# Output projection of the shared stage: three single-pass float32r products of 12-bit halves in place of one float32 product

## The chip, the cores and the metric

One Trainium2 chip, one of its cores. The metric is device time of that core in microseconds (us), the median of the runs shown.

## The reference

One transformer block over x of 2 x 2048 rows and 512 columns (T = 4096 rows):

```python
x = x + attention(layernorm(x))      # 4 x 512 rows, 8 heads of 16, causal
x = x + moe(layernorm(x))            # 8 experts of width 352, top 2, and one shared expert
# the end of attention: out [T, 128] -> out @ OUT_w.T + OUT_b, OUT_w [512, 128]
# the shared expert: silu(xt @ sw1) * (xt @ sw3) @ sw2, and scores = sigmoid(xt @ gate_w.T)
```

In the kernel's reading the batch is 2 x 2048. The change touches `out @ OUT_w.T` and nothing else of the arithmetic.

## The kernel before, in words

Every engine has its own program, written out by hand; they meet in semaphores. Four stages follow each other.

**Projections**, 8 chunks of 512 rows. Per chunk n: VectorE works out the row moments (`moments`, L1143: four BATCH_NORM_STATS2, then a chain of 14 small instructions that wait for each other, the last writes `shift`, L1149). ScalarE normalises with them (`normalise`, L709, four instructions of L714, each reads `shift`). TensorE transposes the normalised rows (`transposes`, L861, 16 instructions of L871), ScalarE copies them out (L722), TensorE projects (`project`, L878). VectorE's order within chunk n is `values(n-1)`, `moments(n+1)`, `rests(n-1)`, `rotate(n)`, `third_parts(n-1)`. In chunk 0 TensorE also transposes OUT_w into bank 3 (L894), and ScalarE copies that bank to `out_wt` (L767), between the Gelu of chunk 0 (L764) and `normalise(1)`; `s_wte` counts that copy, and `transposes(1)` wait for it.

**Attention**, in an order that a planner writes out (`attention_plan`). At its end the plan holds the heads of the next stage: HT (transpose an attention tile of 128 rows, L996, and copy it to `attn_t`, L803), HF (the output product of that tile, L1000, and VectorE's `front`) and HX, for tiles 0 to 2.

**Shared stage**, 32 steps, one for each tile of 128 rows. In step n TensorE does, in this order: `front(n+2)` (the output product, L1025: stationary `attn_t`, moving `out_wt`, 512 columns, bank 7), `turn(n+3)` (transposes the next attention tile, L1017, bank 0), `at(n-1)` (three transposes of the gated rows, L1034), `up(n)` (16 instruction records of L1051, 360 and 352 columns), `down(n-1)` (6 records of L1062). ScalarE: `to_copy(n+3)` (L821, bank 0 to `attn_t`; its semaphore `s_toe` is what `front(n+3)` and the next `turn` wait for), `at_copy(n-1)` (L814), Silu (L836). VectorE: `front(n+2)` (L1217: adds the product to the row of x, L1221 and L1222, its moments and the normalised row `xg`, L1228, some 17 instructions in a chain), `gated(n)` (L1325), `turn(n+1)` (L1214, the transposed tile `xg_t` that `up(n+1)` reads), in some steps a part of the choice of experts (`choose`, L1396 to L1410, in steps 9 to 11, 17 to 19, 25, 26, 28, 30 and 31) or `slots` (L1423 on, in steps 12, 20, 27, 29, 31), then `y(n-1)` (L1340). SyncE issues the transfers in its own order: the attention tile of row n+4 (L481), the normalised row to HBM (L485), a part of an expert's weights (L582 to L588), the same row back in four quarters (L493, after the write has landed), the result row (L577), the row of x (L573).

`x1` is a ring of XR = 6 rows of x; SyncE loads rows 0 to 4 during attention and then row n + XR - 1 in step n, after `y(n-1)`.

**Routed experts**, 71 blocks in a loop, with TensorE busy nearly throughout.

What the change touches, as it stands before:

```python
nc.scalar.copy(out_wt[:, :], psum[:, 3, :]).then_inc(s_wte, 1)                       # L767
nc.scalar.copy(attn_t[:, k % 2, :], psum[:, 0, HP:]).then_inc(s_toe, 1)              # L821
nc.tensor.matmul(psum[:, 7, :], attn_t[:, k % 2, :], out_wt[:, :], start=True, stop=True).then_inc(s_op, 1)   # L1025
```

Of the kernel before, what the change touches and what calls it, by code (L numbers as in the profile page):

```python
# [7 lines left out]
B, S, D = 2, 2048, 512  # L8
# [3 lines left out]
E, H = 8, 352  # L12
TOP_K, ROUTED_SCALE = 2, 2.5
P = 128
# [8 lines left out]
HP = HC * P  # L23
# [8 lines left out]
NA, NBK = 3, 3  # L32

TERMS = [(0, 0), (0, 1), (1, 0), (1, 1), (0, 2), (2, 0)]
KR = len(TERMS) * HD
# [4 lines left out]

fp32, bf16, i32, u16 = mybir.dt.float32, mybir.dt.bfloat16, mybir.dt.int32, mybir.dt.uint16
ALU = mybir.AluOpType
ACT = mybir.ActivationFunctionType
# [174 lines left out]
def program(nc, io):  # L218
    ctx = ExitStack()
    with ctx:  # L220
# [17 lines left out]
        ident, identb = cf("ident"), cbf("ident")  # L238
        out_wt = sb("out_wt", [P, D])
        out_b = sb("out_b", [P, D])  # L240
# [67 lines left out]
        attn_cur = sb("attn_cur", [P, 2, C])  # L308
        attn_t = sb("attn_t", [P, 2, P])
        xg = sb("xg", [P, 2, D])  # L310
# [6 lines left out]
        y_sb = sb("y_sb", [P, 2, D])  # L317
        XR = 6
        x1 = sb("x1", [P, XR, D])

# [10 lines left out]
        per_ei = sb("per_ei", [P, E], i32)  # L331
        per_b = sb("per_b", [P, 3 * NB])
        eid_i = sb("eid_i", [1, NB], i32)
# [9 lines left out]
        by_block = x1f[:, 2 * D:2 * D + NB * E].rearrange("p (b e) -> p b e", e=E)  # L343
        by_block_2 = x1f[:, 2 * D + NB * E:2 * D + 2 * NB * E].rearrange("p (b e) -> p b e", e=E)

        psum = ctx.enter_context(nc.psum_tensor("psum", [P, 8, 512], fp32))
# [9 lines left out]
        s_rld = [sem(f"rope_loaded_{q}") for q in range(QC)]  # L356
        s_wt, s_wte = sem("weights_transposed"), sem("weights_t_ready")
        s_x = [sem(f"x_loaded_{i}") for i in range(2)]
        s_ln = sem("ln_chain")
# [336 lines left out]
        def _(act):  # L696
# [58 lines left out]
            for n in range(NCH):  # L755
                if n >= 1:
                    first_parts(n - 1)
                act.wait_ge(s_pc, n + 1)
                if n == 0:
                    act.wait_ge(s_bp, 16 * 5)  # L760

                if n >= 1:
                    act.wait_ge(s_vp, n)
                nc.scalar.activation(gel_c, psum[:, 6, :], ACT.Gelu, bias=b_proj[:, 2:3]).then_inc(s_gc, 1)  # L764
                if n == 0:
                    act.wait_ge(s_wt, 6)
                    nc.scalar.copy(out_wt[:, :], psum[:, 3, :]).then_inc(s_wte, 1)  # L767
                if n < NCH - 1:
                    normalise(n + 1)
                if n >= 1:  # L770
                    second_parts(n - 1)
                if n < NCH - 1:
                    xt_copy(n + 1)
# [4 lines left out]
            for item in plan:  # L778
# [19 lines left out]
                if item[0] == "HT":  # L798
                    k = item[1]
                    act.wait_ge(s_to, k + 1)  # L800
                    if k >= 2:
                        act.wait_ge(s_op, k - 1)
                    nc.scalar.copy(attn_t[:, k % 2, :], psum[:, k, HP:]).then_inc(s_toe, 1)  # L803

# [3 lines left out]
            def experts(ss, count, u):  # L808
# [7 lines left out]
                def to_copy(n, k):  # L816
                    act.wait_ge(s_to, n + 1)

                    if k >= 2:
                        act.wait_ge(s_op, n - 1)  # L820
                    nc.scalar.copy(attn_t[:, k % 2, :], psum[:, 0, HP:]).then_inc(s_toe, 1)  # L821

# [31 lines left out]
        def _(pe):  # L854
# [7 lines left out]
            def transposes(n):  # L862
# [4 lines left out]
                for c in range(DC):  # L867
                    if n >= 1:
                        pe.wait_ge(s_xte, DC * (n - 1) + c + 1)
                    for t in range(CT):  # L870
                        i = nc.tensor.transpose(psum[:, c, t * P:(t + 1) * P], x_in[n % 2][:, t, c * P:(c + 1) * P], ident)  # L871
                    i.then_inc(s_xt, 1)

            def project(n, which, bank, done):
# [40 lines left out]
            for item in plan:  # L915
# [81 lines left out]
                if item[0] == "HF":  # L997
                    k = item[1]
                    pe.wait_ge(s_toe, k + 1)
                    nc.tensor.matmul(psum[:, k, :], attn_t[:, k % 2, :], out_wt[:, :], start=True, stop=True).then_inc(s_op, 1)  # L1000

# [5 lines left out]
            def experts(ss, count, shared, u):  # L1007
# [11 lines left out]
                def front(n, k):  # L1019
# [3 lines left out]
                    if k >= 1:  # L1023
                        pe.wait_ge(s_x1, n)
                    nc.tensor.matmul(psum[:, 7, :], attn_t[:, k % 2, :], out_wt[:, :], start=True, stop=True).then_inc(s_op, 1)  # L1025

# [89 lines left out]
        def _(dve):  # L1116
# [73 lines left out]
            def third_parts(n):  # L1190
                for a in range(2):
                    dve.wait_ge(s_mid, 2 * n + a + 1)
                    nc.vector.tensor_tensor(parts[n % 2][:, a, 2, :], rest[a], parts[n % 2][:, a, 1, :], ALU.subtract).then_inc(s_parts, 1)

            moments(0)
            dve.wait_ge(s_vpad, 4)
            dve.wait_ge(s_bp, 16 * 5)
            for n in range(NCH):
                if n >= 1:
                    values(n - 1)  # L1200
                if n < NCH - 1:
                    moments(n + 1)
# [32 lines left out]
            for item in plan:  # L1235
# [33 lines left out]
                if item[0] == "RC":  # L1269
# [8 lines left out]
                    if n >= 2:  # L1278
# [3 lines left out]
                                            ALU.mult).then_inc(s_me, 1)  # L1282

                if item[0] == "HF":
                    front(item[1], item[1], item[1])
# [12 lines left out]
            def experts(ss, count, shared, u):  # L1298
# [47 lines left out]
                def step(n, k):  # L1346
                    if shared and n in COUNT_AT:
                        slots(COUNT_AT[n])
                    if shared and k < count - 2:
                        front(n + 2, k + 2, 7)  # L1350
                    if not shared and k < count - 1:
                        turn(n + 1, k + 1)
# [128 lines left out]
```

## Time and profile before

| | us |
|---|---|
| median of 3 runs | 1511.55 (1510.67 to 1513.3) |
| span of the profiled execution | 1524.5 |
| TensorE busy in that span | 1408.5 (92%) |
| VectorE busy | 894.5 (59%) |
| ScalarE busy | 508.0 (33%) |

The profile is of one execution, and of its time only the span is given: it lies 12.95 us above the median of the runs, so a stretch of it may be longer than in a common run. Busy shares are means over stages that have different limits, so the stages are read one by one. In the rows, PE is TensorE, PEld its weight loads, DVE VectorE, ACT ScalarE, POOL GpSimd, SP or SPq SyncE and its transfers.

### The profile page before, as it was taken

What the parts mean: (1) busy time and instruction counts of PE and PEld (TensorE: products, weight loads), DVE (VectorE), ACT (ScalarE), POOL (GpSimd) and SP (SyncE); (2) the same over time, 40 slices, a digit from 0 to 9 for tenths busy, and PEclk for the clock granted to TensorE, in tenths of its full rate; (3) what the DMA queues carried; (4) which work ended last, traced back from release to release, by engine and by line L of the source; (5) the groups of instructions that cost most, each with busy time, mean ns of one, the idle gap of its engine ahead of it and who ended that gap; (6) DMA issues with size and microseconds to landing.
All of it is one profiled execution on the core that took longest, in us unless ns stands there. A gap on an engine that the chain in (4) does not pass through costs nothing.

```text
span 1524.5 us, 21932 instructions
## 1 busy us (share of the span) xinstructions
PE 1408.5 (92%) x6059; PEld 702.8 (46%) x6060; DVE 894.5 (59%) x2655; ACT 508.0 (33%) x1042; POOL 451.3 (30%) x431
## 2 busy tenths in 40 slices
PE   6997899999999999899899983799999999999996
PEld 3552223333433333455455542455555555555553
DVE  4898998888788764678687754233333333333331
ACT  4662466666676777112021121011111111111110
POOL 0000000000000000000222242677777777777771
PEclk9997999999999999999999996899999999999998
DMA  7685310310320000566677661244444444444442
GB/s 223 218 240 158 76 39 4 83 38 5 71 55 5 5 5 24 156 185 183 155 177 187 169 98 47 46 70 69 70 69 69 70 69 69 69 70 69 69 69 35
DMA packets 124855, 136.81 MB, mean 90 GB/s; under 512 B 37047, under 2 KB 86591, under 8 KB 124775
## 3 DMA queue, kind: packets, MB, share of 16 engines
q1 hardware_dynamic: 101350, 96.56, 24.5%
q0 software_dynamic: 21520, 37.84, 14.3%
q10 hardware_dynamic: 1904, 1.46, 0.3%
q8 instruction: 36, 0.59, 0.2%
q14 instruction: 45, 0.36, 0.1%
HBM read 87.03 MB, written 48.83 MB: 89 GB/s over the span
## 4 chain that ended last, share of the span: by engine, by line
PE 72%; DVE 13%; DMA 6%; issue 5%; ACT 2%; POOL 1%; SPq 1%; ACTq 0%; DVEq 0%; POOLq 0%
PE psum L1051 27%; PE psum L1062 14%; PE psum L964 9%; PE psum L946 7%; PE psum L928 6%; PE psum L878 3%; DVE arena L1244 3%; DVE psum L1242 2%; PE psum L1034 2%; DMA xq<-xn_rows 2%; DMA xn_rows<-xg 2%; PE psum L949 1%; DVE stats L1125 1%; PE psum L1025 1%; DMA attn_cur<-attn_rows 1%
## 5 line engine op out<-in xcount | busy, mean ns | idle before, releaser
L1051 PE MATMUL psum<-arena,xg_t 128*128 (+2 forms) x1648 | 519.3, 469 | 20.2 <-DVE xg_t L1214 19.9
L1051 PEld LDWEIGHTS psum<-arena,xg_t 128*128 128x128 f32 x1648 | 312.2, 195 | 182.1 <-issue 31.9
L786 ACT ACTIVATE arena<-psum 128x512 f32<-128x512 f32 (+3 forms) x640 | 303.1, 536 | 170.7 <-PE psum L946 84.6
L648 POOL DMA_INDIRECT table<-const,slot_i x64 | 62.3, 973 | 856.4 <-DVE slot_i L1429 750.2
L664 POOL DMA_INDIRECT xq<-xn_rows,quad_rows x284 | 271.4, 956 | 97.1 <-issue 86.5
L1062 PE MATMUL psum<-arena,act_t 128*128 (+3 forms) x618 | 282.5, 593 | 1.2 <-ACT act_t L814 0.7
L1244 DVE TENSOR_REDUCE arena<-psum 128x1 f32<-128x512 f32 x384 | 251.3, 684 | 40.2 <-PE psum L928 39.6
L928 PE MATMUL psum<-arena 96*128 96x512 bf16 (+3 forms) x640 | 217.9, 359 | 18.3 <-DVE arena L1242 9.9
L1325 DVE TENSOR_TENSOR act_sb<-psum,silu 128x352 f32<-128x352 f32 x103 | 54.0, 524 | 279.4 <-ACT silu L836 195.0
L946 PE MATMUL psum<-arena 99*128 99x512 bf16 (+3 forms) x640 | 214.3, 352 | 1.5 <-ACT arena L786 0.4
L836 ACT ACTIVATE silu<-psum 128x352 f32<-128x352 f32 x103 | 47.7, 463 | 462.8 <-PE psum L1051 419.0
L1062 PEld LDWEIGHTS psum<-arena,act_t 128*128 128x128 f32 (+1 forms) x618 | 117.5, 190 | 121.4 <-issue 100.0
L964 PE MATMUL psum<-arena 128*32 128x512 f32 (+3 forms) x1280 | 150.0, 541 | 2.7 <-ACT arena L797 1.5
L1242 DVE CUSTOM_DVE_ANT_0 psum<-psum,constb 128x128 f32<-128x128 f32 (+3 forms) x256 | 124.0, 497 | 32.2 <-PE psum L928 31.7
L674 POOL DMA_INDIRECT out_rows<-y_sb,row_i x71 | 114.4, 1611 | 91.1 <-issue 66.4
L946 PEld LDWEIGHTS psum<-arena 99*128 99x128 bf16 x640 | 61.1, 97 | 153.1 <-ACT arena L786 112.9
L1342 DVE TENSOR_SCALAR y_sb<-psum,block_pair 128x512 f32<-128x512 f32 x71 | 53.3, 751 | 118.4 <-PE psum L1062 116.8
L814 ACT COPY act_t<-psum 128x384 f32<-128x384 f32 x103 | 49.3, 478 | 205.2 <-PE psum L1062 123.3
L928 PEld LDWEIGHTS psum<-arena 96*128 96x128 bf16 x640 | 62.2, 98 | 102.5 <-DVE arena L1244 40.5
L1214 DVE STREAM_TRANSPOSE xg_t<-xq 128x512 f32<-128x512 f32 x103 | 72.3, 702 | 23.1 <-DMA xq<-xn_rows 17.1
L878 PE MATMUL psum<-arena 128*128 128x512 f32 x192 | 84.0, 593 | 0.0
L1034 PEld LDWEIGHTS psum<-const,act_sb 128*128 128x128 f32 x309 | 40.2, 144 | 53.8 <-issue 45.4
(138 smaller groups left out, 891.7 us busy)
## 6 DMA issues: line engine op xcount, KB each, us to landing
arena<-qk_parts SPq DMA_DIRECT2D x48, 256.0 KB, 6.0
arena<-in_w SPq DMA_DIRECT2D x16, 704.0 KB
arena<-in_x SPq DMA_DIRECT2D x32, 256.0 KB, 4.3
x<-in_x SPq DMA_DIRECT2D x32, 256.0 KB
xn_rows<-xg SPq DMA_DIRECT2D x32, 256.0 KB
xq<-xn_rows SPq DMA_DIRECT2D x128, 64.0 KB
out_rows<-y_sb SPq DMA_DIRECT2D x32, 256.0 KB
qk_parts<-arena SPq DMA_DIRECT2D x16, 384.0 KB, 3.2
```

The costliest lines, as they stand in the source:

```text
L664: nc.gpsimd.indirect_dma_start(out=xq[:, n % 2, g].rearrange("p c b -> p (c b)"), out_offset=None, in_=quarters, in_offset=bass.IndirectOf ...
L674: nc.gpsimd.indirect_dma_start(out=io["out"][:, :], out_offset=bass.IndirectOffsetOnAxis(ap=row_i[:, n:n + 1], axis=0), in_=y_sb[:, n % 2, ...
L786: nc.scalar.activation(probs[:, at_b % PS, d * P:], psum[:, NA + at_b % NBK, 0:CH - d * P], ACT.Exp, scale=float(HD) ** -0.5).then_inc(s_e, 1)
L878: i = nc.tensor.matmul(psum[:, bank, :], w_t[:, which, c, :], xn_t[:, c, :], start=c == 0, stop=c == DC - 1)
L928: ins = nc.tensor.matmul(psum[:, bank, 0:w], stack_q[g][0:KR, j, qt * P:(qt + 1) * P], stack_k[g][0:KR, j, k0:k0 + w], start=True, stop=True)
L946: ins = nc.tensor.matmul(psum[:, bank, 0:CH - d * P], stack_k[g][0:KM, j, kt * P:(kt + 1) * P], stack_q[g][0:KM, j, c * CH + d * P:(c + 1) ...
L964: ins = nc.tensor.matmul(psum[VW * j:VW * (j + 1), 6, d * P:], v_sb[g][:, kt, j, :], probs[:, (at_pv * G + j) % PS, d * P:], start=kt == 0 ...
L1051: i = nc.tensor.matmul(psum[:, bank + k % 2, 0:w], xg_t[:, k % 2, c, :], rhs, start=c == 0, stop=c == DC - 1)
L1062: i = nc.tensor.matmul(psum[:, 6, :], act_t[0:r, k % 2, c, :], rhs, start=c == 0, stop=c == HC - 1)
L1214: nc.vector.transpose(xg_t[:, k % 2].rearrange("p c (g a) -> p g c a", g=QP), xq[:, k % 2]).then_inc(done, 1)
L1242: ins = nc.vector.tensor_tensor_reduce(scores, scores, cbf("mask")[:, CH - w:], 1.0, NEG, ALU.add, ALU.max, top_of)
L1244: ins = nc.vector.tensor_reduce(top_of, scores, AX.X, ALU.max)
```

## The change

The product a x w of float32 values is made of three products of halves. The high half of each operand is its value written out as float32r by ScalarE (12 bits of mantissa), the low half is what VectorE gets when it subtracts the high half from the value still in PSUM. The three products, in the order of `HALVES`, are (a high, w low), (a high, w high), (a low, w high); low x low is left out. They accumulate in the same bank. So each product becomes three matmuls; each copy to `attn_t` and the copy to `out_wt` get a VectorE instruction behind them, and the semaphores that TensorE waits for (`s_toe`, `s_wte`) are now set by VectorE. To make room, `x1` is a ring of 5 rows and `per_b` lies in it.

```diff
+HALVES = [(0, 1), (0, 0), (1, 0)]
+fp32r = mybir.dt.float32r
-        out_wt = sb("out_wt", [P, D])
+        out_wt = sb("out_wt", [P, 2, D], fp32r)
-        attn_t = sb("attn_t", [P, 2, P])
+        attn_t = sb("attn_t", [P, 2, 2, P], fp32r)
-        XR = 6
+        XR = 5
-        per_b = sb("per_b", [P, 3 * NB])
+        per_b = x1f[:, 2 * D + 2 * NB * E:2 * D + 2 * NB * E + 3 * NB]
+        s_oh, s_th = sem("out_weights_first_half"), sem("attention_tile_first_half")
...
-                    nc.scalar.copy(out_wt[:, :], psum[:, 3, :]).then_inc(s_wte, 1)
+                    nc.scalar.copy(out_wt[:, 0, :], psum[:, 3, :]).then_inc(s_oh, 1)
...
-                    nc.scalar.copy(attn_t[:, k % 2, :], psum[:, 0, HP:]).then_inc(s_toe, 1)
+                    nc.scalar.copy(attn_t[:, k % 2, 0, :], psum[:, 0, HP:]).then_inc(s_th, 1)
...
+            def out_product(bank, k):
+
+                for q, (a, b) in enumerate(HALVES):
+                    i = nc.tensor.matmul(bank, attn_t[:, k % 2, a, :], out_wt[:, b, :], start=q == 0, stop=q == 2)
+                return i
...
-                    nc.tensor.matmul(psum[:, 7, :], attn_t[:, k % 2, :], out_wt[:, :], start=True, stop=True).then_inc(s_op, 1)
+                    out_product(psum[:, 7, :], k).then_inc(s_op, 1)
...
+            def out_low():
+                dve.wait_ge(s_oh, 1)
+                nc.vector.tensor_tensor(out_wt[:, 1, :], psum[:, 3, :], out_wt[:, 0, :].bitcast(fp32), ALU.subtract).then_inc(s_wte, 1)
+
+            def turned_low(n, k, bank):
+
+                dve.wait_ge(s_th, n + 1)
+                nc.vector.tensor_tensor(attn_t[:, k % 2, 1, :], psum[:, bank, HP:], attn_t[:, k % 2, 0, :].bitcast(fp32),
+                                        ALU.subtract).then_inc(s_toe, 1)
...
                 if n >= 1:
                     values(n - 1)
+                if n == 0:
+                    out_low()
                 if n < NCH - 1:
                     moments(n + 1)
...
+                if item[0] == "HT":
+                    turned_low(item[1], item[1], item[1])
...
                     if shared and k < count - 2:
                         front(n + 2, k + 2, 7)
+                    if shared and k < count - 3:
+                        turned_low(n + 3, k + 3, 0)
```

The copies and products of the heads (L803, L1000) are changed in the same way.

## Rows read from the trace of the kernel before

**Rows 1.** The page: the span of the profiled execution.
```profile
span 1524.5 us, 21932 instructions
```

**Rows 2.** Busy us of PE, PEld, DVE, ACT, POOL, then PEclk: shared stage, first part.
```profile
618.00:703.00 85.00, 84.71 (x268) 48.56 (x269) 62.99 (x207) 15.70 (x33) 0.00 (x0) 0.98 0.61 183
```

**Rows 3.** Timeline, 0 to 52 us: start, length, engine, line, operation.
```profile
17.54 3.68 PE L871 MATMUL psum<-const,arena 128*128 128x128 f32 x16 [4.09 <-ACT arena L714]
17.62 2.47 DVE L1125 BATCH_NORM_STATS2 stats<-arena 128x6 f32<-128x512 f32 x4 [3.16 <-ACT arena L714]
...
22.99 0.16 DVE L1149 SCALAR_TENSOR_TENSOR shift<-mv,rstd 128x4 f32<-128x4 f32 x1
...
25.99 0.58 ACT L767 COPY out_wt<-psum 128x512 f32<-128x512 f32 x1
26.46 2.93 ACT L714 ACTIVATE arena<-arena,shift,rstd 128x512 f32<-128x512 f32 x4
...
29.28 0.75 DVE L1161 SCALAR_TENSOR_TENSOR arena<-psum,b_proj,arena 128x512 f32<-128x512 f32 x1 [6.13 <-PE psum L878]
...
32.51 1.91 PE L871 MATMUL psum<-const,arena 128*128 128x128 f32 x16
```

**Rows 4.** Chain of waits, 0 to 120 us: start, length, what.
```profile
32.67 1.75 PE psum L871 x16
...
35.31 10.32 PE psum L878 x24
...
55.73 2.94 ACT arena L714 x4
```

**Rows 5.** Timeline of TensorE in the shared stage, steps 0 and 5.
```profile
618.00 0.47 PE L1017 MATMUL psum<-const,attn_cur 128*128 128x128 f32 x1 [2.37 <-DMA attn_cur<-attn_rows]
618.26 6.79 PE L1051 MATMUL psum<-arena,xg_t 128*128 128x360 f32 x16
...
660.32 1.02 PE L1025 MATMUL psum<-out_wt,attn_t 128*128 128x512 f32 x2
661.18 0.27 PE L1017 MATMUL psum<-const,attn_cur 128*128 128x128 f32 x1
...
661.61 4.95 PE L1051 MATMUL psum<-arena,xg_t 128*128 128x360 f32 x16
```

**Rows 6.** Granted clock (PEclk) (the 0.50 and the 1.00) over two short stretches.
```profile
618.00:622.00 4.00, 4.00 (x8) 2.42 (x9) 3.17 (x15) 1.55 (x2) 0.00 (x0) 0.50 0.24 73
622.00:626.00 4.00, 4.00 (x14) 2.15 (x12) 0.41 (x1) 0.46 (x1) 0.00 (x0) 1.00 0.83 253
```

**Rows 7.** Timeline: bf16 products of 512 columns in attention, and weight loads.
```profile
302.18 0.38 PE L928 MATMUL psum<-arena 96*128 96x512 bf16 x1
302.39 0.38 PE L946 MATMUL psum<-arena 99*128 99x512 bf16 x1
...
660.32 0.19 PEld L1025 LDWEIGHTS psum<-out_wt,attn_t 128*128 128x128 f32 x1 [0.24 <-issue]
661.18 0.36 PEld L1034 LDWEIGHTS psum<-const,act_sb 128*128 128x128 f32 x3 [0.29 <-issue]
```

**Rows 8.** Chain of waits, 560 to 960 us: its shares by line.
```profile
by line: PE psum L1051 21.3%; issue 11.0%; PE psum L1062 9.0%; DMA xq<-xn_rows 6.4%; DMA xn_rows<-xg 6.1%; PE psum L964 4.7%; PE psum L946 3.2%; PE psum L1025 3.0%; DMA attn_cur<-attn_rows 3.0%; SPq L493 2.2%; POOL table L648 1.8%; POOL xq 
...
729.49 9.05 DMA xn_rows<-xg
```

**Rows 9.** Timeline of VectorE, shared stage, steps 5, 9, 10 and 12.
```profile
666.15 0.55 DVE L1228 TENSOR_SCALAR xg<-x,mv,rstd 128x512 f32<-128x512 f32 x1
667.10 0.53 DVE L1325 TENSOR_TENSOR act_sb<-psum,silu 128x352 f32<-128x352 f32 x1 [0.40 <-ACT silu L836]
...
704.52 0.69 DVE L1340 TENSOR_TENSOR y_sb<-x,psum 128x512 f32<-128x512 f32 x1
...
713.60 0.68 DVE L1340 TENSOR_TENSOR y_sb<-x,psum 128x512 f32<-128x512 f32 x1
...
722.58 0.21 DVE L1423 TENSOR_TENSOR rank<-psum,const 128x64 f32<-128x64 f32 x1
```

More of the change, by code:

```diff
@@ L802, in _ @@
                         act.wait_ge(s_op, k - 1)
-                    nc.scalar.copy(attn_t[:, k % 2, :], psum[:, k, HP:]).then_inc(s_toe, 1)
+                    nc.scalar.copy(attn_t[:, k % 2, 0, :], psum[:, k, HP:]).then_inc(s_th, 1)
             act.wait_ge(s_pv, n_pv)
@@ L999, in _ @@
                     pe.wait_ge(s_toe, k + 1)
-                    nc.tensor.matmul(psum[:, k, :], attn_t[:, k % 2, :], out_wt[:, :], start=True, stop=True).then_inc(s_op, 1)
+                    out_product(psum[:, k, :], k).then_inc(s_op, 1)
             pe.wait_ge(s_ar, n_a)
```

## The prediction, made before the changed kernel was run

> **What bounds the kernel now.** I read the page first, then the busy time by stage, the chain of waits, and last the timeline of the two stages that the change enters. The profiled execution spans 1524.5 us [rows 1], 12.95 us more than the median of 1511.55. In the shared stage TensorE bounds: from 618 to 703 us it is busy 84.71 of 85 us, VectorE 62.99 [rows 2]. A step is 8.67 us of TensorE work without a hole. Later in the stage transfers and VectorE take the chain over: the write of one normalised row took 9.05 us [rows 8]. The chain shows what a shorter output product can give: L1025 holds 3.0% of 400 us, 12.0 us, and as its piece is 0.86 us (660.32 to 661.18 [rows 5]) it lies on the chain 14 times out of 30. The other 16 are in stretches that something else sets.
>
> In the projection stage the chain is TensorE's too, at the place that matters here: projections of chunk 0, the transposes of chunk 1 at 32.67, the projections at 35.31 [rows 4]. The timeline shows how they are fed. VectorE works out the moments of chunk 1 from 17.62 to 23.15, early, and then stands idle 6.13 us until 29.28. ScalarE copies OUT_w from 25.99 to 26.57 and normalises chunk 1 from 26.46 to 29.39, 3.1 us before TensorE wants it at 32.51 [rows 3].
>
> **The change, part by part.**
>
> *The product, 0.215 us less in a step.* It now takes 0.86 us for 512 columns [rows 5]. The new one is three passes. No row shows a float32r pass. The bound from below is a bf16 pass of 512 columns: 302.18 to 302.39, some 0.215 us, its weight load beside it [rows 7]. The bound from above is a record of the float32 product, half of 0.86: 0.43. I take 0.215, because "single pass" over 512 columns is what the bf16 row is, and a float32 product is four times that. Three make 0.645, a gain of 0.215; at 0.43 they would make 1.29, a loss of 0.43. Over 14 steps the gain is 3.0 us. The Trainium skill (FP8 and Floating Point Precision, TensorE Precision Notes) counts true float32 as four passes and names a reduced one that reads four bytes and cuts them to 22 bits; by it the price is three quarters of the old one, the same 0.645.
>
> *The weight loads, nothing.* A float32 load took 0.19 us and starts with the product before it [rows 7]; 0.19 is under 0.215, so it stays covered, with little to spare. If it is not covered at all, a pass costs 0.215 + 0.19 = 0.405 and the product 1.2, a loss of 0.36 in a step.
>
> *The low half of the tile on VectorE, 0.30 us in a step.* Nearest rows: from PSUM, 352 columns 0.53 and 64 columns 0.21 [rows 9]. Between them 128 columns come to 0.28, and 0.02 to issue. In most steps it is covered. Its copy is done long before. It stands behind the front's `xg`, which ends at 666.70, and before `gated`, which waited 0.40 us for Silu until 667.10 [rows 9]. That hole takes it: `xg` also starts 0.2 earlier, as the product ends earlier. Next in line on VectorE behind it are `gated`, the transposed tile and `y`; TensorE waits for the low half at the next front, some 2 us later. The cover is gone in steps 9 to 11, where VectorE also chooses experts: from `y` at 704.52 to `y` at 713.60 it took 9.08 us [rows 9] against TensorE's 8.67, and TensorE is caught up in step 12 at the ranks read at 722.58. There the low half is on the path twice: +0.6 us. The second such run ends in a wait for a transfer and costs nothing more.
>
> *The low half of OUT_w, +3.3 us at the start.* This is one instruction (0.69 us, as long as `y`'s 512 columns from PSUM [rows 9]), but it stands ahead of `moments(1)` in VectorE's order and waits for ScalarE's copy. The moments that ran in idle time from 17.62 now start when it ends: copy done 26.57, low half 26.62 to 27.31, moments 23.15 - 17.62 = 5.53, so `shift` is ready at 32.84. Normalising takes 2.93, to 35.8, and the transposes that began at 32.51 begin at 35.8 [rows 3]. The 3.1 us of slack are used up by the 6.4 us of delay. Nothing gives this back: each later chunk hangs on the one before, through TensorE or through moments and normalising (the chain has the latter at 55.73 [rows 4]). Queued behind the waiting instruction are `moments(1)` and `rotate(0)`; the latter would start at 32.84 in place of 29.28 and end some 1.6 us later than now, before `values(0)`.
>
> *The clock, +2.0 us.* TensorE now stands idle some 3.1 us there. After a wait of 2.37 us that ended at 618.00, the granted clock was 0.50, that is 1.2 GHz, from 618 to 622 and 1.00, 2.4 GHz, after 622 [rows 6]: 16 records of L1051 took 6.79 where they take 4.95, and the transpose 0.47 for 0.27 [rows 5]. Together 2.0. The bounds are nothing (the clock stays) and that plus 1 us. The 16 transposes at 17.54, after 4.09 us idle, took 3.68 for the 1.91 of the later ones [rows 3], 1.8 more. I take 2.0.
>
> *The heads.* Two of the three early products stand in TensorE's stream in attention: -0.4 us. Their low halves run while VectorE has nothing else. *The ring of 5 rows, nothing:* SyncE waits for the same `y` as before the same transfer, and a row arrives one step, 8.67 us, nearer to its use; still a step and more ahead. `per_b` moves no work.
>
> The sum against the profiled execution: 3.3 + 2.0 - 3.0 + 0.6 - 0.4 = +2.5 us. In a common run, 12.95 us shorter, some of the stretches set by transfers will be TensorE's again; I give it 4 more steps on the chain, -0.9. That makes +1.6, and 1511.55 + 1.6 = 1513.2.
>
> **The rivals.**
>
> *A. A pass costs 0.43 (slower).* Place: every output product. For it: float32 transposes of 128 columns follow each other every (1.91 - 0.27) / 15 = 0.11 us [rows 3], twice 128 columns at 2.4 GHz, so single float32 records stream at half speed. Against it: a transpose has to carry all the bits, a half of 12 has not. It decides from 0.287 a pass on, where three equal the old one. It gives 14 to 18 times 0.43, 6.0 to 7.7, and 3.3 + 2.0 + 0.6 + 0.9: +13 to +14.5, about 1525.5.
>
> *B. The load is not covered (slower).* Place: between the passes. A load of 0.19 in a pass of 0.215 may come late if it can start only with the pass before. Half-covered it costs 0.1 a pass, +0.1 a step in place of -0.215; in all +3.3 + 2.0 + 1.4 + 0.6 = +7.3, 1519. Against it: in the row of the three transposes their loads take 0.36 together, 0.11 apart [rows 7]. The Trainium skill (TensorE: Matmul & The Clock Gate, Part 3) says that loads overlap running matmuls only where the row group differs, which speaks against this change: by it each of the three would pay its load, +0.36 a step. The trace disagrees, with loads of the same rows beside the product.
>
> *C. VectorE becomes the bound (slower).* Place: steps 9 to 12, 17 to 20 and 25 to 31. With 0.30 more and TensorE at 8.45, the transposed tile has 0.3 us left in step 11. If the low half costs 0.6 in place of 0.28, some ten steps lose 0.4 each: +4, 1517.
>
> *D. The clock stays and more steps are TensorE's (less).* 22 steps, -4.7: 3.3 - 4.7 + 0.6 - 0.4 = -1.2, 1510.4.
>
> *E. The delay at the start is not on the path (faster).* Then -3.0 to -4.7 + 0.2: about 1507.8. For it: nothing but that the stage later also waits for VectorE. Against it: the chain.
>
> **How the numbers follow.** My own case 0.31, A 0.12, B 0.05, C 0.15, D 0.25, E 0.12. 0.2% is 3 us, about what a measurement can tell: below 1508.5 is faster, above 1514.6 slower. Slower is A, B, C and a fifth of my own case with its bounds: 0.38. Faster is half of E and a quarter of D: 0.12. The rest, 0.50, is the same. The range runs from E, 1507.5, over C and B to 1521 and leaves out A and the lower half of E.
>
> **What would show it.** Right: the L1025 group has three records of 0.38 us a product, 0.645 from its start to that of L1017, and a step is 8.45 us; DVE's `shift` of chunk 1 is written at 32.8, the PE group of L871 waits for ACT until 35.8, and its 16 records take 3.7 us; everything up to attention is 5 us later than now. Wrong: records of 0.59 us (A), steps over 8.7 (B, C), transposes of chunk 1 at 32.5 (E), or an attention stage that begins at the same time as now.

## The result and the profile after

The changed kernel took 1519.1 us (median of 9 runs, 1515.98 to 1520.93), the kernel before 1512.76 us on the same chip (9 runs, 1509.34 to 1517.66). The ratio is 1.0035, interval 1.002 to 1.005: 5.3 us slower. It is not the quotient of the two medians (1.0042), and all differences below follow the ratios. 5.3 us is inside the stated range, but the sum had said 1.6 us, and the case given the highest chance was no measurable change. The profiled execution took 1520.93 us, at the top of the runs.

The page: the span, and the busy time of each engine.

```profile
span 1519.0 us, 22029 instructions
...
PE 1407.2 (93%) x6091; PEld 712.2 (47%) x6092; DVE 900.9 (59%) x2688; ACT 508.5 (33%) x1042; POOL 451.5 (30%) x431
```

TensorE is busy for 1.3 us less than before, which says little, since a slow clock makes busy time longer. The span cannot be held against the 1524.5 of [rows 1] either, and three executions profiled later show why. They are of low_alone, ring_alone and spread_before, which all have the float32 product. In them the stretch from the first step of the shared stage to the routed experts takes 329 to 330 us, and the rest 560 to 562. In the one profiled execution of the kernel before it was 338.6 and 567.9. So the comparison goes stage by stage.

**The start.** Timeline of the changed kernel, 26 to 46 us, the lines that answer to [rows 3] and [rows 4].

```profile
27.42 0.58 ACT L772 CAST out_wt<-psum 128x512 fp32r<-128x512 f32 x1
...
28.12 0.69 DVE L1208 TENSOR_TENSOR out_wt<-psum,out_wt 128x512 fp32r<-128x512 f32 x1 [13.36 <-ACT out_wt L772]
...
28.73 2.46 DVE L1136 BATCH_NORM_STATS2 stats<-arena 128x6 f32<-128x512 f32 x4
...
34.09 0.16 DVE L1160 SCALAR_TENSOR_TENSOR shift<-mv,rstd 128x4 f32<-128x4 f32 x1
...
34.29 2.93 ACT L719 ACTIVATE arena<-arena,shift,rstd 128x512 f32<-128x512 f32 x4 [6.29 <-DVE shift L1160]
...
37.27 3.58 PE L876 MATMUL psum<-const,arena 128*128 128x128 f32 x16 [3.17 <-ACT arena L719]
...
41.63 4.89 PE L889 MATMUL psum<-arena 128*128 128x512 f32 x11
```

VectorE stood idle for 13.36 us until OUT_w's copy came, and only then began the moments (28.73) that ran at 17.62 before. `shift` is written at 34.09, ScalarE had waited 6.29 for it, TensorE 3.17. The projections of chunk 1 start at 41.63. In the kernel before they started at 35.15:

```profile
35.15 10.46 PE L878 MATMUL psum<-arena 128*128 128x512 f32 x24
```

That is 6.48 later. Of these, 1.43 were there ahead of the change: the copy itself ran at 27.42 in place of 25.99. This belongs to the execution, as changed_again will show. The other 5.05 are 3.33 of wait and 1.72 of slow TensorE work, nearly all in the transposes (3.58 for 1.91). The clock over the same stretch (us in the window, then busy time of PE, PEld, DVE, ACT, POOL; then PEclk):

```profile
32.00:40.00 8.00, 4.83 (x18) 3.31 (x17) 5.74 (x18) 4.10 (x6) 0.00 (x0) 0.84 0.01 2
40.00:50.00 10.00, 10.00 (x32) 5.44 (x32) 7.62 (x29) 5.73 (x10) 0.00 (x0) 0.96 0.78 264
```

0.84 where it was 1.00 in the kernel before: after a gap of 3.17 us the clock was below 2.4 GHz for part of the stretch (0.50, that is 1.2 GHz, from 38 to 40 us).

The delay is still there when attention begins. Its first bf16 products, before and after:

```profile
125.14 0.33 PE L928 MATMUL psum<-arena 96*128 96x128 bf16 x3
...
131.67 0.33 PE L939 MATMUL psum<-arena 96*128 96x128 bf16 x3
```

Counted from the copy of OUT_w this is 99.15 us before and 104.25 after, 5.1 more.

**A step of the shared stage.** Timeline of the changed kernel, 657 to 669 us, with TensorE's weight loads:

```profile
657.22 2.74 PE L1073 MATMUL psum<-arena,act_t 128*128 128x512 f32 x6
...
657.43 0.28 DVE L1213 TENSOR_TENSOR attn_t<-psum,attn_t 128x128 fp32r<-128x128 f32 x1
...
657.92 0.52 DVE L1350 TENSOR_TENSOR act_sb<-psum,silu 128x352 f32<-128x352 f32 x1 [0.21 <-ACT silu L841]
...
659.38 0.19 PEld L882 LDWEIGHTS psum<-out_wt,attn_t 128*128 128x128 f32 x1 [0.24 <-issue]
659.40 1.25 PE L882 MATMUL psum<-out_wt,attn_t 128*128 128x512 f32 x3
...
659.80 0.42 PEld L882 LDWEIGHTS psum<-out_wt,attn_t 128*128 128x128 f32 x2 [0.24 <-issue]
...
660.49 0.27 PE L1028 MATMUL psum<-const,attn_cur 128*128 128x128 f32 x1
...
668.98 0.27 PE L1028 MATMUL psum<-const,attn_cur 128*128 128x128 f32 x1
```

A step is 668.98 - 660.49 = 8.49 us, against 8.67 [rows 5]: 0.17 less, not 0.215. Two loads take 0.42 together, 0.23 from one to the next, though one alone takes 0.19. The group of the product's records as a whole (min/median/max ns):

```profile
L882 PE MATMUL psum<-out_wt,attn_t x96: 389/397/804, 605.6 to 897.4; 128*128 128x512 f32 x96
```

Three records stand for a product. Their length is modelled and they overlap, so the first of them does not mark the start of the product: it is drawn at 659.40, 1.09 us ahead of L1028, while the product ahead of it (six records of L1073 from 657.22, 0.43 apart) still runs until 659.80. From there to 660.49 is 0.69, and the step says the same: 0.86 - 0.17 = 0.69. The low half of the tile takes 0.28 and the wait ahead of `gated` fell from 0.40 [rows 9] to 0.21, so the hole that was to take it took it.

**The choice of experts.** Timeline of VectorE and TensorE around the two reads of the ranks:

```profile
711.64 0.69 DVE L1365 TENSOR_TENSOR y_sb<-x,psum 128x512 f32<-128x512 f32 x1
...
721.03 0.68 DVE L1365 TENSOR_TENSOR y_sb<-x,psum 128x512 f32<-128x512 f32 x1
...
729.61 0.69 DVE L1365 TENSOR_TENSOR y_sb<-x,psum 128x512 f32<-128x512 f32 x1
730.21 0.22 DVE L1450 TENSOR_TENSOR rank<-psum,const 128x64 f32<-128x64 f32 x1
...
730.58 0.30 PE L1028 MATMUL psum<-const,attn_cur 128*128 128x128 f32 x1 [1.66 <-DVE rank L1450]
...
808.92 0.45 PE L1028 MATMUL psum<-const,attn_cur 128*128 128x128 f32 x1 [1.90 <-DVE rank L1450]
...
809.80 6.17 PE L1062 MATMUL psum<-arena,xg_t 128*128 128x360 f32 x16
```

and the third `y` in the kernel before:

```profile
721.98 0.69 DVE L1340 TENSOR_TENSOR y_sb<-x,psum 128x512 f32<-128x512 f32 x1
```

From `y` to `y` VectorE takes 9.39 us in the first of these steps, 0.31 more than before [rows 9], while TensorE wants 8.49. In the next it takes 8.58 for 8.38 (721.98 - 713.60), 0.20 more. The 0.20 are what the low half adds from start to start where VectorE has no hole. The step before has, besides, a pause of another length among the small instructions of the moments. The wait at the ranks of step 12 is 1.66 us in place of 0.65, at those of step 20 1.90 in place of 1.19. After the second the clock was lower in this execution: 16 records of L1062 took 6.17 for 4.95, and the granted clock was 0.72 from 810 to 814 us.

### The profile page after: what moved, and what is told of

Read it like the earlier page. It is cut to its first block, busy times and chain, and to the rows that moved or that the text cites. A ratio compares the mean times of both kernels' runs of the same rounds, so it can differ in the third digit from the quotient of the medians.

```text
span 1519.0 us, 22029 instructions
## 1 busy us (share of the span) xinstructions
PE 1407.2 (93%) x6091; PEld 712.2 (47%) x6092; DVE 900.9 (59%) x2688; ACT 508.5 (33%) x1042; POOL 451.5 (30%) x431
## 4 chain that ended last, share of the span: by engine, by line
PE 73%; DVE 14%; DMA 6%; issue 3%; ACT 2%; SPq 1%; POOL 1%; ACTq 0%; DVEq 0%; POOLq 0%
PE psum L1062 28%; PE psum L1073 14%; PE psum L975 9%; PE psum L957 7%; PE psum L939 6%; DVE arena L1267 3%; PE psum L889 3%; DVE psum L1265 2%; PE psum L1045 2%; DMA xn_rows<-xg 2%; DMA xq<-xn_rows 2%; DVE stats L1136 1%; ACT arena L719 1%; PE psum L876 1%; DMA attn_cur<-attn_rows 1%
## 5 line engine op out<-in xcount | busy, mean ns | idle before, releaser
L1062 PE MATMUL psum<-arena,xg_t 128*128 (+2 forms) x1648 | 520.2, 470 | 19.9 <-DVE xg_t L1237 19.5
L1062 PEld LDWEIGHTS psum<-arena,xg_t 128*128 128x128 f32 x1648 | 313.2, 195 | 181.6 <-issue 32.3
L1073 PE MATMUL psum<-arena,act_t 128*128 (+3 forms) x618 | 282.5, 593 | 1.2 <-ACT act_t L819 0.7
L1073 PEld LDWEIGHTS psum<-arena,act_t 128*128 128x128 f32 (+1 forms) x618 | 117.7, 191 | 121.2 <-issue 99.9
L1237 DVE STREAM_TRANSPOSE xg_t<-xq 128x512 f32<-128x512 f32 x103 | 72.3, 702 | 20.6 <-DMA xq<-xn_rows 13.5
```

The costliest lines, as they stand in the source:

```text
L1062: i = nc.tensor.matmul(psum[:, bank + k % 2, 0:w], xg_t[:, k % 2, c, :], rhs, start=c == 0, stop=c == DC - 1)
L1073: i = nc.tensor.matmul(psum[:, 6, :], act_t[0:r, k % 2, c, :], rhs, start=c == 0, stop=c == HC - 1)
L1237: nc.vector.transpose(xg_t[:, k % 2].rearrange("p c (g a) -> p g c a", g=QP), xq[:, k % 2]).then_inc(done, 1)
```

## The experiments

Each ratio is against the kernel before, run on the same chip in the same rounds. The first four shared one chip (before: 1512.77 us, 34 runs), the next four a second (1524.07 us, 35 runs), the last four a third (1512.45 us, 35 runs). Where two forms did not share a chip, only their ratios are compared.

### late_low: the change, with the low half of OUT_w behind the moments

```diff
                 if n >= 1:
                     values(n - 1)
-                if n == 0:
-                    out_low()
                 if n < NCH - 1:
                     moments(n + 1)
+                if n == 0:
+                    out_low()
```

> The changed kernel with one thing moved: the low half of OUT_w is made after the moments of chunk 1, not before them. Theory (the start of the projection stage costs 3.3 us of waiting and 1.7 us of slow clock, and the rest of the change gives about as much as it takes): the transposes of chunk 1 follow the projections of chunk 0 with no wait, 16 in 1.9 us, and the time is 5.0 us below the changed kernel, 1514, within 2 us of the kernel before. Rival (the start is made up for later, and the shared stage holds the loss): within 1 us of the changed kernel, 1519, with the stage still 5 us earlier. Second rival (the shared stage gains the 3 us of the forecast in every run): 1510, faster than before.

1510.43 us, ratio 0.9994 (0.9979 to 1.001), 6.2 us below the change by the ratios, where 5.0 were expected. Timeline of late_low, 12 to 46 us:

```profile
27.21 0.58 ACT L772 CAST out_wt<-psum 128x512 fp32r<-128x512 f32 x1
...
27.68 2.93 ACT L719 ACTIVATE arena<-arena,shift,rstd 128x512 f32<-128x512 f32 x4
...
27.82 0.69 DVE L1208 TENSOR_TENSOR out_wt<-psum,out_wt 128x512 fp32r<-128x512 f32 x1 [4.48 <-ACT out_wt L772]
...
33.73 1.91 PE L876 MATMUL psum<-const,arena 128*128 128x128 f32 x16
...
36.37 10.04 PE L889 MATMUL psum<-arena 128*128 128x512 f32 x23
```

The same subtraction at nearly the same time, 27.82, but nobody waits: ScalarE normalises from 27.68, the transposes take 1.91 and have no wait ahead of them. The loss is gone, at the start of attention too: from the copy of OUT_w to the first bf16 product it is 99.23 us.

### low_alone: the kernel before, with that wait and subtraction alone

```diff
-                    nc.scalar.copy(out_wt[:, :], psum[:, 3, :]).then_inc(s_wte, 1)
+                    nc.scalar.copy(out_wt[:, :], psum[:, 3, :]).then_inc(s_oh, 1)
...
+                if n == 0:
+                    dve.wait_ge(s_oh, 1)
+                    nc.vector.tensor_tensor(y_sb[:, 1, :], psum[:, 3, :], out_wt[:, :], ALU.subtract).then_inc(s_wte, 1)
```

It stands ahead of `moments(1)`; nothing reads what it writes.

> The kernel before with one thing added: in chunk 0 VectorE waits for the copy of OUT_w and subtracts it from PSUM ahead of the moments of chunk 1, into rows that nothing reads; the products stay float32. Theory: the wait before the transposes of chunk 1 is 3.2 us, the 16 transposes take 3.6 in place of 1.9, and the whole is 5.0 us above the kernel before, 1517.8. Rival (start made up for later): no difference, 1512.8. If only the wait counts and the clock costs nothing in the end: +3.3, 1516.

1517.30 us, ratio 1.0033 (1.0019 to 1.0046): 5.0 us, all of the change's loss without any of the change. Timeline of low_alone, 12 to 46 us:

```profile
27.79 0.69 DVE L1204 TENSOR_TENSOR y_sb<-psum,out_wt 128x512 f32<-128x512 f32 x1 [13.27 <-ACT out_wt L768]
...
36.94 3.49 PE L872 MATMUL psum<-const,arena 128*128 128x128 f32 x16 [3.17 <-ACT arena L715]
...
41.30 4.89 PE L879 MATMUL psum<-arena 128*128 128x512 f32 x11
```

The same chain and the same wait of 3.17 us, and here too the slow transposes, 3.49. From the copy of OUT_w to the first bf16 product it is 104.27 us, as in the change.

### filled_hole: the change, with TensorE kept busy through the gap

```diff
+                if n == 0:
+                    pe.wait_ge(s_wte, 5)
+                    for q in range(28):
+                        nc.tensor.transpose(psum[:, 7, q % 4 * P:(q % 4 + 1) * P], ident, ident)
```

The 28 transposes stand behind the projections of chunk 0 and write a bank that nobody reads.

> The changed kernel with 28 further transposes of the identity on TensorE after the projections of chunk 0, written to a bank that is not yet in use, some 28 x 0.11 = 3.1 us of work that nothing needs, so that TensorE is not idle while VectorE and ScalarE catch up. Theory (1.7 of the 5.0 us are the clock): the granted clock stays at 1.00, the 16 transposes take 1.9 us, and the time is 1.7 us below the changed kernel, 1517.4. Rival (the clock costs nothing, or falls whatever TensorE does): the same as the changed kernel, 1519. It takes nothing from the 3.3 us.

1514.58 us, ratio 1.0015 (1.0004 to 1.0027). Timeline of filled_hole, 12 to 46 us:

```profile
34.48 3.22 PE L916 MATMUL psum<-const 128*128 128x128 f32 x28
...
37.83 1.97 PE L876 MATMUL psum<-const,arena 128*128 128x128 f32 x16
...
40.52 5.74 PE L889 MATMUL psum<-arena 128*128 128x512 f32 x13
```

The transposes of chunk 1 start as late as without the filling, and run at full speed. Against the copy of OUT_w (27.97 here, 25.99 before) the projections are 40.52 - 35.15 - 1.98 = 3.4 us late: the wait alone is left. Against the change's 1.0035 the ratio came down by 3.0 us, where 1.7 were expected; the intervals leave room for both. Against late_low on the same chip it is 3.2 us up (1.0015 and 0.9994), the price of the wait. So the medians speak for a cost of the clock that the filling takes away, though each has an interval of some 2 us to either side. The trace alone does not show it: one clock that stayed up does not prove that the filling kept it up, and changed_again, below, has the same without any filling.

### ring_alone: the kernel before, with the ring of 5 rows and `per_b` in it

```diff
-        XR = 6
+        XR = 5
```

> The kernel before with x1 as a ring of 5 rows and per_b in it, and nothing else. Theory: no difference to the kernel before, within 0.1%, and no VectorE wait for a row of x. Rival (a row of x comes late behind the slow transfers of steps 12 to 14, and again later): VectorE waits for x before L1221, 1 to 3 us in total, and as much in the time.

1511.78 us, ratio 1.0 (0.9986 to 1.0014). Nothing, as the prediction had it.

### four_products: late_low with the fourth product, low by low

```diff
-HALVES = [(0, 1), (0, 0), (1, 0)]
+HALVES = [(1, 1), (0, 1), (0, 0), (1, 0)]
...
-                    i = nc.tensor.matmul(bank, attn_t[:, k % 2, a, :], out_wt[:, b, :], start=q == 0, stop=q == 2)
+                    i = nc.tensor.matmul(bank, attn_t[:, k % 2, a, :], out_wt[:, b, :], start=q == 0, stop=q == 3)
```

> late_low with a fourth pass, low x low, in every output product. It shows what one pass costs and on how many steps the output product is on the path. Theory (a pass is 0.215 us, and some 18 of 30 steps are set by TensorE): a step is 8.71 us in place of 8.49, and the time is 3 to 4.5 us above late_low, 1514. If a pass costs 0.43, a step is 8.92 and the time 8 us up. Rival (stretches set by transfers and VectorE absorb what TensorE gains or loses): steps of 8.71, and less than 1.5 us in the whole.

1523.62 us, ratio 0.9997 (0.9985 to 1.001). Timeline of TensorE in four_products, 661 to 671 us:

```profile
661.28 0.66 PEld L882 LDWEIGHTS psum<-out_wt,attn_t 128*128 128x128 f32 x3 [0.24 <-issue]
...
662.21 0.27 PE L1028 MATMUL psum<-const,attn_cur 128*128 128x128 f32 x1
...
670.93 0.27 PE L1028 MATMUL psum<-const,attn_cur 128*128 128x128 f32 x1
```

The step is 8.73 us (five steps from 653.48 to 697.13), 0.24 more than late_low's 8.49. So the fourth pass costs 0.24, and four of them cost 0.06 more than the float32 product's 0.86, 0.23 each; three take 0.69. The three loads in 0.66 keep the same distance, (0.66 - 0.19) / 2 = 0.235. That settles the size of a pass. It does not settle what paces it: passes and loads alternate, so they keep one distance whichever of them sets it, and no run leaves a load out. The total hardly moved: 0.24 in each of 32 products makes 7.7 us, and by the ratios four_products is 0.5 to 2 us above late_low (0.9994 and, again, 0.9984), on other chips and with intervals that overlap. 7.7 us would have shown; the 3 us at the lower end of what was expected cannot be excluded.

### no_tile_low: late_low without the low half of the tile

```diff
-HALVES = [(0, 1), (0, 0), (1, 0)]
+HALVES = [(0, 1), (0, 0), (0, 1)]
```

and without `turned_low`, with ScalarE's copy setting `s_toe` again. Its result leaves out the product with the low half of the tile.

> late_low without VectorE's low half of the attention tile; the third product takes the high half of the tile with the low half of OUT_w again, so TensorE's work is the same and the low half of the tile is missing from the result. It gives the price of the VectorE instruction alone. Theory (it is covered in most steps and on the path twice in each run of choosing steps): steps of 8.49, the waits for the ranks read in steps 12 and 20 are 0.9 and 0.4 to 1.2 in place of 1.67 and 1.52, and the time is 1.2 to 2 us below late_low, 1509. Rival (it is covered everywhere): within 0.5 us of late_low. Rival (VectorE sets most steps): 5 us below.

1522.37 us, ratio 0.9992 (0.9975 to 1.0009). The step stays at 8.49 us and the wait ahead of `gated` is back at 0.40. The waits for the ranks are 0.93 and 1.04 us. The first is 1.66 to 1.68 in all five traces with three passes, one low half and this order of choosing, so the low half is what lengthened it. From step 9 to step 12 TensorE takes 26.9 us without the low half, 27.6 with it in late_low, and 27.1 with the float32 product. The second wait is 1.18 to 1.90 in the five traces, and less sure. In the total the 1.2 to 2 us that were expected between the two forms are not seen: 0.9992 stands between late_low's 0.9994 and 0.9984.

### double_tile_low: late_low with a second, smaller subtraction in each step

```diff
+                nc.vector.tensor_tensor(silu_low[:, k % 2, :], psum[:, bank, HP:HP + 88], attn_t[:, k % 2, 0, 0:88].bitcast(fp32), ALU.subtract)
```

> late_low with one more VectorE subtraction in every step, of 88 columns from PSUM, some 0.24 us, ahead of the low half. Theory (only the choosing steps feel VectorE): +0.24 twice in each of two runs of steps, +1 us, the waits in steps 12 and 20 some 0.5 longer each; plain steps go on at 8.49 or a little more, since the 0.2 us of idle VectorE time before the gated product is used up: the time is 1 to 3 us above late_low. Rival (VectorE is at its limit in every step): +0.24 x 30, 7 us.

1524.41 us, ratio 1.0009 (0.9991 to 1.0026). Timeline of VectorE in double_tile_low, 667 to 669 us:

```profile
667.97 0.24 DVE L1214 TENSOR_TENSOR silu_low<-psum,attn_t 128x88 f32<-128x88 f32 x1
...
668.12 0.28 DVE L1215 TENSOR_TENSOR attn_t<-psum,attn_t 128x128 fp32r<-128x128 f32 x1
...
668.45 0.53 DVE L1352 TENSOR_TENSOR act_sb<-psum,silu 128x352 f32<-128x352 f32 x1
```

Now the hole ahead of `gated` is full (no wait is shown), and a plain step is still 8.49. Of the waits for the ranks, the first is as in late_low (1.62 us) and the second longer than in any other trace (2.14). No low half, one, and one with 88 columns more stand at 0.9992, 0.9994 and 0.9984 (late_low, on other chips), and 1.0009. The longest form is the slowest, as it would be with VectorE as the bound, but the intervals of all four overlap.

### spread_choice: late_low with the choice of experts spread out

```diff
-CHOOSE = {9: ((0, 0),), 10: ((0, 1),), 11: ((0, 2),), 17: ((1, 0),), 18: ((1, 1),), 19: ((1, 2),),
+CHOOSE = {9: ((0, 0),), 11: ((0, 1),), 12: ((0, 2),), 17: ((1, 0),), 19: ((1, 1),), 20: ((1, 2),),
...
-COUNT_AT = {12: 0, 20: 1, 27: 2, 29: 3, 31: 4}
-PUT_AT = {0: 12, 1: 20, 2: 27}
+COUNT_AT = {13: 0, 21: 1, 27: 2, 29: 3, 31: 4}
+PUT_AT = {0: 13, 1: 21, 2: 27}
```

> late_low with the choice of experts spread: its second part in steps 11 and 19 and not 10 and 18, its third in steps 12 and 20, the ranks in steps 13 and 21 and the pairs written from there. VectorE then has a step between two choosing ones to catch up. Theory: TensorE's waits for the ranks read (1.67 and 1.52 in late_low) shrink to under 0.8, the clock does not fall there, and the time is 1 to 3 us below late_low, 1508.5, and so below the kernel before by more than 0.1%. Rival: the scattered pairs, one step later, run into the transfers of the next steps, and the wait of 6.7 us in step 14 grows by as much: no gain.

1520.20 us, ratio 0.9966 (0.9949 to 0.9983), the fastest against its own chip. The waits for the ranks are 1.03 and 1.03 us, not under 0.8 as expected.

### late_low_again, changed_again: both forms side by side

> late_low once more, so that it stands beside the changed kernel and the spread choice on one chip: its ratio was 0.9994 to 1510.4 us on one chip, and the kernel before alone took 1512.8 on that chip and 1524.1 on the next. Theory (three passes with the low half of OUT_w out of the way are worth a little, 0 to 3 us): a ratio of 0.998 to 1.0, and 0.0033 below the changed kernel on the same chip.

> The changed kernel as it is, again, beside late_low. Theory: 5.0 us above late_low, a ratio of 0.0033 more, whatever the chip; of these, 4.8 to 5.2 are already there when the projections of chunk 1 begin. If the start is made up for on a chip where transfers are slower: less than 2.5 us.

late_low_again took 1509.14 us, ratio 0.9984 (0.997 to 0.9997), changed_again 1516.90 us, 1.0027 (1.0014 to 1.0041). The placement of one instruction is worth 0.0043, 6.5 us, on one chip. Timeline of changed_again, 12 to 46 us:

```profile
26.01 0.58 ACT L772 CAST out_wt<-psum 128x512 fp32r<-128x512 f32 x1
...
32.69 0.16 DVE L1160 SCALAR_TENSOR_TENSOR shift<-mv,rstd 128x4 f32<-128x4 f32 x1
...
35.87 1.97 PE L876 MATMUL psum<-const,arena 128*128 128x128 f32 x16 [3.17 <-ACT arena L719]
...
38.56 7.89 PE L889 MATMUL psum<-arena 128*128 128x512 f32 x18
```

Here the copy runs at 26.01, as it did before (25.99), so this trace needs no correction: the transposes start at 35.87, 3.36 us after the 32.51 of [rows 3]. And after the same gap of 3.17 us they took 1.97, and the clock was 1.00 from 32 to 40. From the copy of OUT_w to the first bf16 product it is 102.60 us, 3.4 more than the 99.2 of late_low_again, and that much is the wait alone. So the wait is certain, and the slow clock behind it came in two of three executions (3.58 in the first trace of the change, 3.49 in low_alone).

The traces also tell how far the gain of the product reached. Starts of the attention tile's transpose in the shared stage, in us from the first one, as read from the timelines:

| | step 9 | step 11 | step 12 | step 13 | step 14 | step 20 | routed experts |
|---|---|---|---|---|---|---|---|
| ring_alone (float32 product) | 77.7 | 95.0 | 104.8 | 113.5 | 125.5 | 180.2 | 328.8 |
| late_low_again | 76.5 | 93.5 | 104.2 | 112.7 | 126.5 | 181.1 | 328.65 |
| late_low | 76.5 | 93.5 | 104.2 | 112.7 | 128.0 | 183.9 | 331.3 |
| changed_again | 77.4 | 94.4 | 105.0 | 113.6 | 128.7 | 183.2 | 330.8 |

By step 11 the three passes are 1.5 us ahead of the float32 product (in changed_again 0.9 of it went to a slow first step). Step 12 waits for VectorE, and 0.6 is left. Step 14 waits for its attention tile, and there nothing can be seen of the 0.6: the tile comes at 125.5, 128.5 and 129.3 in the traces of ring_alone, low_alone and the kernel before, and at 126.5 to 128.7 in the five with halves and the same order of choosing. That the transfer ends at a time of its own is read from this overlap; no run holds the transfer fixed. The steps after that are 8.5 or 8.67 apart again, and the end is the same within what executions of one form differ by.

### spread_again, spread_before: the spread with and without the halves

spread_before is the kernel before with the diff of spread_choice, its float32 product kept.

> spread_choice again, beside late_low: its ratio was 0.9966. Theory (the spreading itself is worth 3 us by the ranks' waits and the clock): 2 to 4 us below late_low and the ratio again 0.996 to 0.998. Rival (that run was luck of the transfers): the same ratio as late_low.

> The kernel before with the choice of experts spread in the same way and the float32 product kept. VectorE has 0.3 us less to do in a step and TensorE 0.17 more than in spread_choice. Theory (the spread removes the place where the low half of the tile was on the path, so that it is worth less without that half): a ratio of 0.998 to 1.0, above that of spread_choice by 0.001 to 0.002, which is then the worth of the three passes. Rival (the spread alone makes the gain): the same ratio as spread_choice.

spread_again took 1509.23 us, ratio 0.9976 (0.996 to 0.9992), spread_before 1509.31 us, 0.9977 (0.996 to 0.9993). So the rival of spread_before came out: the spread alone brings 3.5 us on the kernel before, and the three passes add nothing to it that the runs could tell. Between late_low_again and spread_again, on this same chip, the spread is worth 1.2 us, less than the 2 to 4 expected and not clear of the intervals. The first wait for the ranks, first in spread_again:

```profile
732.03 0.30 PE L1028 MATMUL psum<-const,attn_cur 128*128 128x128 f32 x1 [1.01 <-DVE rank L1450]
```

and in spread_before:

```profile
733.94 0.30 PE L1017 MATMUL psum<-const,attn_cur 128*128 128x128 f32 x1 [0.48 <-DVE rank L1423]
```

1.01 us with the halves, 0.48 without. From step 9 to step 13 TensorE takes 35.47 us with the halves and 35.61 without: of the 0.7 us that four shorter products bring, 0.1 is left. How the spread helps the kernel before stays open: its waits at the ranks (0.48 and 1.54 us) are together no shorter than ring_alone's (0.65 and 0.48), and its shared stage in the one trace is no shorter either (329.25 us against 328.8).

## Why the prediction was partly right

- **The wait at the start, +3.3: right.** 3.36 in changed_again, 3.33 in the first trace; changed_again has `shift` at 32.69 and the transposes at 35.87, for 32.8 and 35.8 in the forecast. The loss follows the instruction when it is put alone into the kernel before (1.0033) or moved behind the moments (0.9994, 0.9984). Nothing gave it back, as stated: the delay is whole at the start of attention (104.25 and 104.27 us from the copy, for 99.15 to 99.23). Rival E (not on the path) is out.
- **The clock, +2.0: right in size where it happens, wrong as a certainty.** 1.7 and 1.6 us in two executions, nothing in a third. Its share of the median is known roughly: low_alone and changed_again are 5.0 and 6.5 us above the forms without the gap, filled_hole is 3.2, and 3.3 is the wait, so some 2 to 3 us are left for the clock, with intervals as wide as that. One of the two rows that the forecast rested on was misread. The gap of 4.09 us did not make the 16 transposes at 17.54 slow, for the first ones, ahead of that gap, had the same pace (0.22 us apart, where later ones are 0.11 apart):

```profile
10.66 2.79 PE L859 MATMUL psum<-const,arena 128*128 128x128 f32 x12 [10.66 <-DMA arena<-in_wc]
```

  The slow first step of the shared stage [rows 6] carries the 2.0 alone.
- **The product, -0.215 a step: the right mechanism, too large.** A pass is 0.23 to 0.24 us, not 0.215, so three take 0.69 and a step gains 0.17. Rival A (0.43) is out, and so is B's 0.1 us a pass. Where the 0.02 over the bf16 row comes from is open: from a load that is not quite covered (0.19 and 0.045 to the next), or from the pass itself. The Trainium skill (TensorE: Matmul & The Clock Gate, Part 3) says that loads overlap running matmuls only where the row group differs. The 0.24 that the fourth pass added does not bear that out here: with its load of 0.19 paid in full it would be 0.4.
- **Fourteen steps, and four more, of it on the path: the step that failed.** I took L1025's share of the chain as the number of steps in which a shorter product shortens the kernel. 1.5 us are gained by step 11, as 9 steps should bring. But the gain earned before a later wait, for VectorE at step 12 and, as far as one trace of each form shows it, for the tile at step 14, does not outlast it. A share of the chain tells what the time is spent on, and it is no promise that time taken from it stays gone. In all, the forecast had -3.7 us for everything but the start (-3.0 - 0.9 + 0.6 - 0.4); late_low has -0.9 and -2.4. This is where 2 of the 3.7 us between +1.6 and +5.3 come from. The rest lies within the interval of the ratio (3.0 to 7.6 us). That 1519.1 fell into a range of 13.5 us is in part luck: the range was wide enough to hold a term that was 2 us wrong.
- **The low half on VectorE, 0.30, hidden in plain steps, 0.6 in the first run of choosing steps: right.** 0.28 long, 0.20 from start to start, and 27.6 us from step 9 to step 12 where no_tile_low has 26.9. *"The second such run ends in a wait for a transfer and costs nothing more"* was wrong: it ended in a wait for the ranks, 1.90 us, and in this execution in a slow clock. Rival C (VectorE the bound) holds at the waits for the ranks and not in plain steps, which stay at 8.49 even in double_tile_low. Its price in the total is too small for the runs: no_tile_low and double_tile_low, on one chip, are 0.0017 apart with intervals that overlap.
- **The heads, -0.4: not seen.** From the first bf16 product to the first step of the shared stage it takes 493.9 to 494.0 us in five traces with the halves (the change twice, late_low twice, filled_hole) and 492.9 to 494.5 in three with the float32 product (before, low_alone, ring_alone).
- **The ring, nothing: right** (1.0).
- **Rival D** (22 steps, clock stays) would have made late_low some 4.5 us faster than before. It is 0.9 and 2.4.

The forecast put 0.50 on no measurable change and 0.38 on slower, and slower it was. The start was priced rightly at 5 us; most of what was to pay for it was not there. The fastest forms tried are 0.24 to 0.34% under the kernel before (spread_choice, spread_again), and spread_before reaches the same with the float32 product. With the moments first, the three passes are 0.06 and 0.16% under the float32 product; with the spread as well, the two cannot be told apart. That a half has 12 bits of mantissa is a premise of the change that no run here shows; none of the sums rests on it.

## What to carry to other kernels

An instruction that waits, put into an in-order engine ahead of work that had been running early in idle time, moves all of that work: here 0.69 us of VectorE cost 5 us, and one place further down it cost nothing. Before counting a gain by the share of the chain, look for the next wait that may end at a time of its own (a transfer, a slower engine), because what is gained before it may be gone behind it: here 1.5 us were. And price a new kind of pass by adding one more of it: the fourth pass told 0.24, where the row of another type had said 0.215.

## What was not expected of the hardware

- A float32r pass of 512 columns paced at 0.235 us, though 512 columns take 0.215 in the bf16 row and a load takes 0.19.
- The same gap of 3.17 us ahead of the same transposes left the clock lower in two executions and at 1.00 in a third; filled_hole, with no gap, had fast transposes as well. In attention the first trace of the change has a clock of 0.77 and 0.81 in two windows where the kernel before has 1.00 and 1.00. Such a dip, behind a gap of no more than 1.08 us, goes with neither form: between 336 and 350 us seven of the fourteen traces have one, ring_alone's and low_alone's among them, and the other seven, late_low_again's and filled_hole's among them, have none. Windows of the changed kernel, columns as above:

```profile
342.50:346.50 4.00, 3.26 (x20) 1.20 (x21) 2.70 (x15) 0.56 (x2) 0.00 (x0) 0.77 0.10 21
346.50:350.50 4.00, 4.00 (x23) 1.45 (x21) 3.03 (x14) 2.08 (x5) 0.00 (x0) 0.81 0.07 15
```

  So one execution's clock is no price; it takes several.
- The kernel before took 1512.8, 1524.1 and 1512.5 us on three chips. In the traces of the second the shared stage lasts 338 to 343 us, on the two others 326 to 331 (333 in the first trace of the change): the waits of TensorE for the attention tile, without the one at step 0, add up to 8 to 14 us there, elsewhere to 5 to 8. So every ratio is to the kernel before on the same chip.
